# Two groups instead of three: reordering TensorE's work inside one attention head

## The reference

```python
x1 = layernorm(x)
q, k, v = heads(x1 @ Wq), heads(x1 @ Wk), heads(x1 @ Wv)      # 2 x 16 heads x 1024 x 16
w = softmax(quadrant_weights)
k_eff1 = w[0] * k1 + w[1] * k2 ; k_eff2 = w[2] * k1 + w[3] * k2
attn = softmax((q1 @ k_eff1.T + q2 @ k_eff2.T) * scale)        # 1024 x 1024 for each head
x = x + (attn @ v) @ Wo
```

## Time and profile before

| | |
|---|---|
| median of 3 runs | 1677.78 us (1677.19 to 1680.77) |
| the profiled execution, first to last instruction | 1676.8 us |
| head 0 starts / head 10 starts / head 30 starts | 82.67 / 202.50 / 443.19 us |
| last `normalise` of the first attention ends | 472.80 us |
| one head inside the loop, and one across the loop's turn | 12.00 / 12.17 us |
| granted TensorE clock over that stretch | 1.00 (2.4 GHz) |

### The profile page before, as it was taken

The page is one execution under the profiler, slowest core; times in us unless marked ns, Lnnn a source line. Parts: engine busy times, 40 slices in busy tenths (PEclk is TensorE's granted clock), DMA queues, the critical chain, the costliest instruction groups (busy, mean ns, idle before and its releaser), DMA issues. The chain is left out here.

```text
span 1676.8 us, 31751 instructions
## 1 busy us (share of the span) xinstructions
PE 1555.5 (93%) x10885; PEld 1112.7 (66%) x10886; DVE 961.9 (57%) x1728; ACT 581.3 (35%) x1135; POOL 402.1 (24%) x557
## 2 busy tenths in 40 slices
PE   7999999999989926999999999999989979999996
PEld 6734343434457715777777777776657779999995
DVE  7688888888779876121112211278879863444443
ACT  3277777777745501111111111133346510000000
POOL 2000000000122103133212211156652113333331
PEclk9999999999999968999999999999999999999998
DMA  2112221111411111134322331110025136666674
GB/s 77 40 44 66 59 59 43 46 42 47 164 33 39 51 45 37 18 100 107 101 47 73 100 91 16 15 52 2 2 67 174 50 104 183 185 186 183 173 180 118
DMA packets 89079, 134.93 MB, mean 80 GB/s; under 512 B 17568, under 2 KB 66080, under 8 KB 88832
## 3 DMA queue, kind: packets, MB, share of 16 engines
q1 hardware_dynamic: 73824, 113.05, 21.4%
q0 software_dynamic: 15168, 20.72, 7.7%
HBM read 98.00 MB, written 20.84 MB: 71 GB/s over the span
## 5 line engine op out<-in xcount | busy, mean ns | idle before, releaser
L2215 DVE TENSOR_REDUCE mx<-ps 128x1 f32<-128x1024 f32 x256 | 300.5, 1216 | 58.6 <-PE ps L2310 58.3
L1363 PE MATMUL ps<-xTe,wide 128*128 128x320 f32 x1024 | 277.4, 433 | 1.8 <-DVE hTe L1432 1.7
L1363 PEld LDWEIGHTS ps<-xTe,wide 128*128 128x128 f32 x1024 | 194.3, 190 | 82.3 <-DVE hTe L1432 2.2
L1432 DVE TENSOR_TENSOR hTe<-prT,ps 128x320 f32<-128x320 f32 x128 | 62.3, 488 | 213.6 <-ACT prT L1404 203.3
L2109 ACT ACTIVATE wide<-ps 128x512 f32<-128x512 f32 x256 | 139.0, 598 | 65.3 <-PE ps L2319 65.3
L2109 ACT ACTIVATE turns_of_use<-ps 128x512 f32<-128x512 f32 x256 | 139.3, 600 | 59.1 <-PE ps L2319 59.0
L2319 PE MATMUL ps<-QS,KS 99*128 99x512 bf16 x512 | 153.8, 381 | 0.7 <-ACT turns_of_use L2109 0.3
L1526 PEld LDWEIGHTS ps<-xw_all,w1t 128*128 128x128 f32 x1248 | 145.3, 192 | 3.2 <-DVE hTm L1571 1.3
L1526 PE MATMUL ps<-xw_all,w1t 128*128 128x128 f32 x1248 | 145.8, 275 | 1.0 <-DVE hTm L1571 1.0
L1404 ACT ACTIVATE prT<-ps 128x320 f32<-128x320 f32 x128 | 56.0, 437 | 261.9 <-PE ps L1363 252.5
L1543 PE MATMUL ps<-wide,hTm 128*128 x624 | 141.0, 379 | 0.0
(11 more groups left out here) (312 smaller groups left out, 2310.4 us busy)
## 6 DMA issues: line engine op xcount, KB each, us to landing
w1t<-in_L_ffn_w SPq DMA_DIRECT2D x39, 1024.0 KB
wide<-in_L_ffn_gate_weight SPq DMA_DIRECT2D x8, 1024.0 KB
wide<-_L_ffn_ff_pre_act_weight SPq DMA_DIRECT2D x8, 1024.0 KB
wide<-L_ffn_ff_post_act_weight SPq DMA_DIRECT2D x8, 1024.0 KB
wide<-in_L_ffn_w SPq DMA_DIRECT2D x1, 8192.0 KB, 27.4
QS<-wide SPq DMA_DIRECT2D x192, 32.0 KB, 1.9
KS<-wide SPq DMA_DIRECT2D x192, 32.0 KB, 2.0
VS<-V_all SPq DMA_DIRECT2D x32, 128.0 KB, 2.1
```

Source lines behind the costliest of these rows:

```text
L1363: ins = pe.matmul(ps[:, 3 + 2 * (q % 2) + n, 0:HC], wt[:, k, f * P:f * P + P], xTe[:, k, hf * HC:hf * HC + HC], start=(k == 0), stop=(k == ...
L1432: v.tensor_tensor(hTe[:, f, hf * HC:hf * HC + HC], sgt[:, q % 2, :], ps[:, 4 + 2 * (q % 2), 0:HC], ALU.mult).then_inc(f_m.sem, 1)
L2215: v.tensor_reduce(mx[:, s, t:t + 1], ps[:, 2 * (t % 2):2 * (t % 2) + 2, :], AX.XY, ALU.max).then_inc(h_rm.sem, 1)
```

## The change

Four things change, all in the first attention.

1. `weigh` is called twice in a head, for tiles 0 to 3 and for tiles 4 to 7, not three times. Tiles 4 to 7 of the head before come after the first `scores_t`.
2. The scores for the maxima are issued one tile at a time between the `scores_t`, not two at a time; `turn_max` and `turn_sums` each have a `scores_t` between them. The new order: `scores_t` 0; `weigh` 4 to 7 of the head before; `scores_t` 1; score 0; `scores_t` 2, 3; score 1; `scores_t` 4; `turn_max`; `scores_t` 5; `turn_sums`; `scores_t` 6; score 2; `scores_t` 7; score 3; `scores_t` 8, 9; `weigh` 0 to 3; score 4; `scores_t` 10, 11; score 5; `scores_t` 12 to 14; score 6; `scores_t` 15; score 7. In heads 30 and 31 the first matmuls of the cross attention move with these places.
3. ScalarE's `evac` of the head before comes after exponential 0, not after exponential 2.
4. GpSimd's split uses four operations, not five, and waits for its own results twice, not four times; the parts are positive, and the ones in `KS` become minus ones.

```diff
--- before.py
+++ after.py
@@ -213,7 +213,7 @@
         rec = sbA("rec", [P, 2, 4])
         EB = [(4, 5, 7)[i % 3] for i in range(63)] + [5]
         back_to = lambda i: next(d for d in range(1, 64) if EB[(i - d) % 64] == EB[i])
-        TWO_ONES = float(np.array(0x3F803F80, np.uint32).view(np.float32))
+        TWO_MINUS_ONES = float(np.array(0xBF80BF80, np.uint32).view(np.float32))
 
         a_xn = sig("a_xn")
         a_tr = sig("a_tr")
@@ -2021,7 +2021,7 @@
             c(pool.memset(onesb[:], 1.0))
             c(pool.memset(root[:], -0.5))
             c(pool.memset(eps[:], LN_EPS))
-            pool.memset(KS[96:99, :, :].rearrange("p n s -> p (n s)").bitcast(F32), TWO_ONES).then_inc(ones_set, 1)
+            pool.memset(KS[96:99, :, :].rearrange("p n s -> p (n s)").bitcast(F32), TWO_MINUS_ONES).then_inc(ones_set, 1)
             pool.wait_ge(ones_set, 1)
             pool.iota(iota_b[:], pattern=[[1, P]], base=0, channel_multiplier=0, allow_small_or_imprecise_dtypes=True)
             pool.iota(tiles_b[:], pattern=[[1, NY]], base=0, channel_multiplier=0, allow_small_or_imprecise_dtypes=True)
@@ -2048,13 +2048,13 @@
                 pool.wait_ge(h_rm.sem, h_rm.upto(n))
                 pool.wait_ge(h_mt.sem, h_mt.upto(n - 2))
                 none = zeros[:, 0:1].to_broadcast([P, TB])
-                c(pool.tensor_tensor(mpart[:, s, 0, :], none, mx[:, s, :], ALU.subtract))
-                c(pool.tensor_tensor(mleft[:, 0, :], mx[:, s, :], mpart[:, s, 0, :], ALU.add))
-                c(pool.tensor_tensor(mpart[:, s, 1, :], none, mleft[:, 0, :], ALU.subtract))
-                c(pool.tensor_tensor(mleft[:, 1, :], mleft[:, 0, :], mpart[:, s, 1, :], ALU.add))
-                pool.tensor_tensor(mpart[:, s, 2, :], none, mleft[:, 1, :], ALU.subtract).then_inc(h_mp.sem, 1)
-
-            with c.fori(B * H // 2, 2 * 4) as i:
+                c(pool.tensor_tensor(mpart[:, s, 0, :], mx[:, s, :], none, ALU.add))
+                pool.tensor_tensor(mleft[:, s, :], mx[:, s, :], mpart[:, s, 0, :], ALU.subtract)
+                c(pool.tensor_tensor(mpart[:, s, 1, :], mx[:, s, :], mpart[:, s, 0, :], ALU.subtract))
+                pool.tensor_tensor(mpart[:, s, 2, :], mleft[:, s, :], mpart[:, s, 1, :], ALU.subtract)\
+                    .then_inc(h_mp.sem, 1)
+
+            with c.fori(B * H // 2, 2 * 2) as i:
                 for s in range(2):
                     split_max(2 * i + s, s)
             pool_first_rows(pool, c)
@@ -2114,10 +2114,10 @@
                 act.copy(Osb[:], ps[:, 6, 0:256]).then_inc(h_ev.sem, 1)
 
             def head(n, hh, first=False):
-                exps(n, hh, 0, 3)
+                exps(n, hh, 0, 1)
                 if not first:
                     evac(n - 1)
-                exps(n, hh, 3, 16)
+                exps(n, hh, 1, 16)
 
             act.wait_ge(a_p3.sem, a_p3.upto(NP - 1))
             for n in range(4):
@@ -2355,8 +2355,7 @@
 
                 def ahead_scores(t):
                     if ahead:
-                        for tt in (t, t + 1):
-                            scores(n + 2, s2, tt)
+                        scores(n + 2, s2, t)
                     elif (hh, t) == (2, 0):
                         pe_first_rows(pe)
                     elif (hh, t) == (2, 2):
@@ -2370,30 +2369,36 @@
                     elif (hh, t) == (3, 6):
                         pe_first_scores(pe)
 
-                scores_t(n, sl, 0, 3)
+                scores_t(n, sl, 0, 1)
                 if not first:
-                    weigh(n - 1, (sl + 3) % 4, 6, 8)
-                scores_t(n, sl, 3, 4)
+                    weigh(n - 1, (sl + 3) % 4, 4, 8)
+                scores_t(n, sl, 1, 2)
                 if ahead:
                     pe.wait_ge(h_ld[s2].sem, h_ld[s2].upto(i + (hh + 2) // 4))
                 ahead_scores(0)
-                scores_t(n, sl, 4, 6)
+                scores_t(n, sl, 2, 4)
+                ahead_scores(1)
+                scores_t(n, sl, 4, 5)
                 if not (last and hh == 3):
                     turn_max(n + 1, (hh + 1) % 2)
+                scores_t(n, sl, 5, 6)
                 if not first:
                     turn_sums(n - 1)
-                scores_t(n, sl, 6, 8)
+                scores_t(n, sl, 6, 7)
                 ahead_scores(2)
-                scores_t(n, sl, 8, 11)
+                scores_t(n, sl, 7, 8)
+                ahead_scores(3)
+                scores_t(n, sl, 8, 10)
                 pe.wait_ge(h_no.sem, h_no.upto(n - 1))
                 pe.wait_ge(h_mc.sem, h_mc.upto(n if last and hh == 3 else n + 1))
-                weigh(n, sl, 0, 3)
-                scores_t(n, sl, 11, 12)
+                weigh(n, sl, 0, 4)
                 ahead_scores(4)
+                scores_t(n, sl, 10, 12)
+                ahead_scores(5)
                 scores_t(n, sl, 12, 15)
-                weigh(n, sl, 3, 6)
+                ahead_scores(6)
                 scores_t(n, sl, 15, 16)
-                ahead_scores(6)
+                ahead_scores(7)
 
             pe.wait_ge(ones_set, 1)
             for n in range(2):
@@ -2411,7 +2416,7 @@
                     head(4 * i + hh, hh, i)
             for hh in range(4):
                 head(B * H - 4 + hh, hh, B * H // 4 - 1, False, True)
-            weigh(B * H - 1, 3, 6, 8)
+            weigh(B * H - 1, 3, 4, 8)
             turn_sums(B * H - 1)
             pe_cross(pe, 0)
             meet(pe, 2)
```

## The result

| | before | after |
|---|---|---|
| median | 1677.67 us (4 runs) | 1686.39 us (1685.55 to 1687.03, 4 runs) |
| profiled span | 1676.8 us | 1685.1 us |
| ratio to before | | 1.0048, 95% interval 1.0035 to 1.006 |

The change makes the kernel slower by 8.7 us. The forecast was +5.0, with 1676 to 1691 as its range.

The account below looks back on a forecast made before the run. TensorE's written order was taken to set the pace, with ScalarE's exponentials late after the change. +1.9 us for 29 heads, -1.4 for head 0 and +4.5 for heads 30 and 31 gave +5.0: 1682.8 us, range 1676 to 1691.

Parts of the forecast that it names:

- The chain in front of `weigh` 4 to 7: From `scores_t` 10 through exponentials 10 to 15 to that `weigh`: 3.58 us, making a head 12.07.
- the fourth head: Every fourth head uses bank 5 twice at its end, so `scores_t` 15 waits for exponential 13: about 0.1 us more.
- the point whose margin the prediction put at under 0.1: `weigh` 0 to 3 waits for exponential 7: ScalarE done after 4.24 us, TensorE there after 4.30.
- GpSimd's split: Four operations take 0.96 us, not 1.31; the new place of `turn_max` covers them by about 0.8, so worth nothing.
- the gain on offer: TensorE's own work per head falls to 11.39 us, 0.65 less than now; over 31 heads 20 us.
- Scores one by one: Single tiles cost TensorE nothing, and VectorE has 2 us of slack a head: -0.1 to +0.1 us a head.
- Head 0: First head, one group of four instead of two of three: -1.4 us, bounds -1.1 and -1.6.
- Heads 30 and 31: Last two heads, with cross attention matmuls where scores were; exponentials come later: +4.5 us, bounds +2.5 and +5.5.
- rival 1: In the loop, TensorE's sum holds: a head takes 11.4 us, time about 1658 to 1662; chance 11%.
- Rival 2: Loop as forecast, but slack after head 31 absorbs the end: +0.5 to +2 us, 1679; chance 12%.
- Rival 3: On ScalarE, long queues of exponentials run slower than threes: 1688 to 1700 us; chance 5%.
- Rival 4: Row of maxima or keys land late, so `scores_t` 0 or score 0 waits: 1695 us at 0.5 a head; chance 4%.

Follow-up runs that it names:

- short exponentials: The changed kernel with exponentials 10 to 15 taking only 256 of 512 columns from head 4 on: 1678.47 us, 1.0001 of the kernel before.
- the moved `scores_t`: The changed kernel with `scores_t` 1 in front of `weigh` 4 to 7 and `evac` behind exponential 1: 1683.16 us, 1.0014 of the kernel before.
- the old order at the end: The changed kernel with TensorE's and ScalarE's order of the kernel before in heads 30 and 31 only: 1682.87 us, 1.001 of the kernel before.
- pairs: The changed kernel with the scores for the maxima again issued two tiles at a time: 1702.43 us, 1.0149 of the kernel before.
- second execution: The changed kernel run once more, unchanged: 1688.48 us, 1.0041 of the kernel before.
- evac late: The changed kernel with `evac` of the head before behind exponential 2 again, not exponential 0: 1696.95 us, 1.0092 of the kernel before.
- old split: The changed kernel with the maxima again split in five operations with four waits: 1687.72 us, 1.004 of the kernel before.

## Why the prediction was right, and where a size was off

*The chain in front of `weigh` 4 to 7* decided, and its terms were right: 3.58 laid out, 3.60 measured; 8.49 and 8.50 for TensorE's part; so 12.07 laid out for an ordinary head and 12.10 measured. For the fourth head 0.1 more was laid out, and it takes 0.21 more. The loop's turn is not the reason: head 27, which leaves the loop into a head that is written out, takes 12.30 too, while in the kernel before that step takes 12.00 and a turn 12.26. Its rows show about half of the 0.21:

```profile
420.88 0.39 PE L2319 MATMUL ps<-QS,KS 99*128 99x512 bf16 x1 [0.16 <-ACT wide L2109]
...
421.96 1.45 PEld L2329 LDWEIGHTS ps<-wide,VS 128*32 128x32 f32 x32 [0.53 <-ACT wide L2109]
```

`scores_t` 15 waits for bank 5. `scores_t` 10 started at 418.27, so the chain is 421.96 - 418.27 = 3.69, the 0.1 that was laid out. The other 0.11 lies in front of it: `weigh` 0 to 3 starts 6.31 behind the group before it and not 6.19. That is the point whose margin the prediction put at under 0.1; what it waits for there wasn't tried. Over heads 1 to 29 the mean is 12.13, and the term in the sum was +1.9 us and is +2.7. The short exponentials show that ScalarE's rate is the cause, and the moved `scores_t` shows the place.

*GpSimd's split*: 0.96 laid out, 0.92 measured, worth nothing in the new order, as forecast. Its cover in front of `turn_max` was laid out at 0.8 and is 1.37. In the old order it is worth 0.04 a head, since score 3 takes the wait over, so the 0.38 that I counted in "the gain on offer" was not a price that the kernel paid for the split alone.

*VectorE* was put at nothing ("Scores one by one", between -0.1 and +0.1 a head, with 2 us of slack). In the changed kernel that does no harm, because the wait for ScalarE is longer. But the short exponentials show that the slack is not there across a group of four: with ScalarE's chain out of the way, the reductions hold a head at 11.87, 0.5 over TensorE's 11.39. So "the gain on offer" of 20 us was never on offer with this order.

*Head 0*: -1.4 forecast, -1.37 measured.

*Heads 30 and 31*: +4.5 forecast within +2.5 to +5.5, +6.35 measured, outside these bounds. This is the term that was mis-sized. What I had not in it is the clock. The group that waits for ScalarE ran at 0.52 for 3.48 us where it takes 1.87 at 1.00, so 1.6 of the 1.9 us are the clock. Without it the end is +4.7. Its first two waits are +2.0 and +1.8, against +1.9 each. The last is +1.4 and not +0.9, since exponential 15 is not queued behind the others:

```profile
477.45 0.60 ACT L2109 ACTIVATE wide<-ps 128x512 f32<-128x512 f32 x1 [0.40 <-PE ps L2319]
```

`scores_t` 15 stands behind the first scores of the cross attention, and ScalarE waits for it, so the chain from 474.00 to 478.10 is 4.10 and not 3.58. What is lost again before the last `normalise` is 0.6 and not 0.2. The two errors nearly cancel, which is luck.

*What the forecast had at nothing*: head 0 started 1.10 us later. In the first projection stage, which is the same code, sixteen matmuls took 6.10 us and not 4.98. The busy-time view gives 1.00 as the clock there for both, but the spacing of these equal matmuls speaks for the lower level at first: they start 0.43 apart, as from 14.53 to 14.95, and 0.216 apart later, where sixteen of them fill 3.62 us in both kernels. Between 16.00 and 17.00 the view counts six of them in the kernel before and four in the changed one. At 0.21 more for each, 1.1 us means that the step up came about five matmuls later; why it did is open. In the other runs the first `turn_max` stands anywhere from 77.53 to 80.62 us with the same code ahead of it, so this belongs to the execution and not to the change. With it at zero the sum would be +7.7 to the end of the first attention. If this reading is right, 1.1 and 1.6 of the +8.8 are TensorE's clock, which the forecast didn't have, and 6.1 stand against its +5.0. The median is 3.7 over the forecast and lies within 1676 to 1691 because that range was wide.

*The rivals*: rival 1 needed a shorter chain; it is as long as its rows said, and with shorter exponentials a head is still 11.93, not 11.4. Rival 2 is out by the old order at the end. Rival 3: six queued exponentials run at the pace of the threes, 3.04 = 0.60 + 5 x 0.488. Rival 4: no wait of TensorE on SyncE in the loop. The estimate of 0.52 us a step, worked out in the prediction from the figures of the Trainium skill ("ScalarE: Activation LUTs", section "What ACT_TABLE_LOAD costs"), is not what six in a row show here: they are 0.488 apart.

## What to carry to other kernels

When a hand-written order is regrouped, lay out for each waiting instruction what runs between it and the last thing it waits for: here 1.83 us from `scores_t` 15 to its `weigh` became 0.87 of TensorE's own work, and 0.25 us saved at a switch cost about 0.7 of standing still (12.07 - 11.39). A stall shown in a trace is a gain only as far as the next wait in the same cycle lies behind it. When one chain is cut, look for the next: with ScalarE's shortened, VectorE's held the head, only 0.2 us lower. In this kernel finer interleaving, with the shorter split, was worth 7.5 to 10 us; fewer, longer groups made it slower, with pairs and with single tiles.

## What the runs showed of the hardware

Within the heads of the first attention the granted clock fell only at the end of four executions, all of kernels with two groups. From the last `turn_max` to the last `normalise` the mean clock is 0.95 in the changed kernel, in its second execution, and with evac late or the old split; it is 1.00 in the eight others, among them the two-group kernels with more cover, with short exponentials, with pairs and with the old order at the end. Where it falls varies. In the second execution of the changed kernel the group that had run at 0.52 took 1.87 us at 1.00, and the lower clock came 3.5 us later, over three `scores_t`, a turn of rows and part of the next group:

```profile
460.68:462.55 1.87, 1.87 (x32) 0.94 (x33) 0.00 (x0) 0.44 (x1) 0.03 (x1) 1.00 0.22 69
462.55:466.06 3.51, 2.10 (x13) 0.76 (x9) 1.14 (x4) 3.30 (x7) 0.00 (x0) 1.00 0.00 0
466.06:468.08 2.02, 2.02 (x8) 0.85 (x8) 0.69 (x1) 0.77 (x3) 1.26 (x1) 0.59 0.00 0
468.08:470.79 2.71, 2.71 (x34) 1.20 (x33) 0.00 (x0) 0.84 (x2) 0.00 (x0) 0.68 0.00 0
```

In front of it TensorE had been busy for 2.10 of 3.51 us. In both cases a run of short waits for ScalarE stood ahead, and in the loop, where 237.40 of 243.07 us are busy, the clock stayed at 1.00. Waits cost twice there: once by themselves, and once by the work behind them. But such a stretch does not always bring the clock down. The same one in the first execution of the changed kernel was followed by work at 1.00:

```profile
465.14:468.66 3.52, 2.10 (x13) 0.76 (x9) 1.14 (x4) 3.30 (x7) 0.00 (x0) 1.00 0.00 0
```

What decides between the two is open, and which of the waits has to go for the clock to stay wasn't tried by itself.
